# Attention scores as twelve 32-row products in four row groups, in place of four 96-row products

## What is computed

```python
q = _split_heads(query @ Wq.T + bq)
k = _split_heads(key @ Wk.T + bk)
v = _split_heads(value @ Wv.T + bv)
score = jnp.einsum('bhqd,bhkd->bhqk', q, k) * SCALE
attn = jax.nn.softmax(score, axis=-1)
out = jnp.einsum('bhqk,bhkd->bhqd', attn, v)
```

## Time and profile before

| | before |
|---|---|
| median of 3 runs | 1943.54 us (1938.99 to 1945.22) |
| span of the profiled execution | 1941.7 us |
| instructions | 46658 |
| attention, first to last score product | 55.1 us to 1420 us |

### The profile page before, as it was taken

How to read it: one execution, slowest core, us unless ns; L and a number is a source line. 1 busy time by engine, 2 the same in 40 slices (tenths; PEclk the granted TensorE clock), 3 DMA queues, 4 the chain that set the end, 5 groups by cost and what they waited for, 6 DMA issues and landing times. The chain is left out here.

```text
span 1941.7 us, 46658 instructions
## 1 busy us (share of the span) xinstructions
PE 1876.6 (97%) x18832; PEld 1777.8 (92%) x18832; DVE 1468.1 (76%) x2796; ACT 1136.1 (59%) x1921; POOL 652.9 (34%) x643
## 2 busy tenths in 40 slices
PE   7899999999999999999999999999879889999998
PEld 5899999999999999999999999999867789999998
DVE  6777778777777777777777778777788567766667
ACT  2465666666566656666665566656765436665552
POOL 3222223322222323222223232223031126888860
PEclk9899999999999999999999999999989799999999
DMA  8666666666666666666666666667510236666633
GB/s 272 170 155 162 156 174 169 164 157 159 161 153 167 170 167 167 157 158 157 159 167 164 170 165 162 156 163 189 149 60 23 76 118 209 225 220 218 229 115 132
DMA packets 146790, 313.85 MB, mean 162 GB/s; under 512 B 57888, under 2 KB 77216, under 8 KB 143120
## 3 DMA queue, kind: packets, MB, share of 16 engines
q1 hardware_dynamic: 140672, 295.03, 56.2%
q0 software_dynamic: 4752, 13.38, 2.3%
q10 hardware_dynamic: 1152, 2.47, 0.5%
HBM read 134.20 MB, written 18.35 MB: 79 GB/s over the span
## 5 line engine op out<-in xcount | busy, mean ns | idle before, releaser
L453 ACT COPY a_pT<-a_pst 128x512 f32<-128x512 f32 x768 | 421.2, 583 | 409.0 <-PE a_pst L963 409.0
L459 ACT ACTIVATE a_probs<-a_probs,a_nmax 128x1601 f32<-128x1601 f32 x256 | 418.8, 1636 | 140.0 <-DVE a_probs L636 139.8
L636 DVE TENSOR_SCALAR_CACHE_REDUCE a_probs<-a_pss 128x1608 f32<-128x1608 f32 x256 | 467.3, 1825 | 12.8 <-PE a_pss L952 12.3
L963 PE MATMUL a_pst<-a_id,a_probs 128*128 128x128 f32 (+1 forms) x3328 | 452.6, 275 | 13.7 <-ACT a_pT L453 11.5
L963 PEld LDWEIGHTS a_pst<-a_id,a_probs 128*128 128x128 f32 (+1 forms) x3328 | 382.8, 141 | 51.1 <-issue 21.0
L355 POOL TENSOR_TENSOR a_tick<-a_tick 128x1 f32<-128x1 f32 x62 | 12.0, 193 | 953.4 <-DMA a_raw<-in_ctxT 892.1
L654 DVE TENSOR_SCALAR a_khi<-a_psk,a_bk 128x402 fp32r<-128x402 f32 x250 | 158.5, 634 | 142.9 <-PE a_psk L917 141.3
L360 POOL TENSOR_TENSOR a_clo<-a_raw,a_chi 128x402 fp32r<-128x402 f32 x240 | 247.0, 1060 | 4.8
L952 PE MATMUL a_pss<-a_kst,a_bd 96*128 96x402 f32 x1024 | 240.7, 357 | 6.4 <-DVE a_v L661 5.6
L915 PE MATMUL a_pso<-a_whi,a_chi 128*128 128x256 f32 (+1 forms) x806 | 241.9, 300 | 0.0
L917 PE MATMUL a_pso<-a_whi,a_clo 128*128 128x256 f32 (+1 forms) x806 | 227.2, 282 | 0.0
(11 more groups left out here) (251 smaller groups left out, 3511.7 us busy)
## 6 DMA issues: line engine op xcount, KB each, us to landing
a_kst<-a_khi SPq DMA_DIRECT2D x1008, 100.5 KB, 2.6
a_kst<-a_klo SPq DMA_DIRECT2D x504, 100.5 KB, 2.6
a_raw<-in_ctxT SPq DMA_DIRECT2D x60, 804.0 KB, 5.5
f_gur<-in_wgu SPq DMA_DIRECT2D x24, 1408.0 KB, 6.2
f_dr<-in_wd SPq DMA_DIRECT2D x24, 768.0 KB, 7.2
a_bd<-q_scr SPq DMA_DIRECT2D x192, 32.0 KB, 2.0
e_big<-ys_scr SPq DMA_DIRECT2D x8, 512.0 KB, 6.7
a_pT<-in_ctxT SPq DMA_DIRECT2D x2, 1608.0 KB, 9.3
```

The costliest lines, as they stand in the source:

```text
L453: nc.scalar.copy(pT[:, p % HALF, 4 * i:4 * i + 4, :], ps_t[:, i % 2, :].rearrange("p (t q) -> p t q", q=P)).then_inc(t_copied_act, 1)
L459: nc.scalar.activation(pr, pr, ACT.Exp, bias=nmax[:, b, p:p + 1], scale=-1.0, accum_out=esum[:, b, p:p + 1]).then_inc(probs_ready, 1)
L636: nc.vector.tensor_scalar(probs[:, p % 2, :].rearrange("p (b k) -> p b k", b=QK), ps_s[:, :, 0:KQ], -SCALE, None, ALU.mult, ALU.min, accum ...
L963: mm = nc.tensor.transpose(ps_t[0:r, i % 2, (t % 4) * P:(t % 4 + 1) * P], probs[:, p % 2, t * P:t * P + r], a_id_sb[:])
```

## The change

`k_hi` and `k_lo` become the two parts of one tile `k_sb`. The stacked keys become `kq`: row group q (rows 32q to 32q+31) holds key quarter q of each pair, high and low part side by side, 402 columns each. `bd` holds high and low queries side by side, and the same 32 rows in each of the four row groups. `scores` makes three products (high query x high key, high x low, low x high) for each quarter, product by product over the four quarters, each on its own 32 rows and into its quarter's bank, accumulating there.

A batch's key copies go from 48 transfers of 32 rows x 804 columns to 32 of 32 rows x 2 x 402 columns. The queries go from six transfers from memory to four, and three copies of 32 rows x 2048 words (256 KB each) inside the core's memory are added (`spread_queries`), for which SP waits until the four have landed. Two waits of the first batch on stored queries go away, the tiles lie elsewhere in memory, and `bd` is zeroed over 128 rows x 4096 words, where it was 96 x 2048.

```diff
-STACK = 3 * 32
+ROWS = 2 * HD
 PIECES = 2
-COPIES = 16 * 3 * HALF
+COPIES = 16 * (QK // PIECES) * HALF
+PRODUCTS = ((0, 0), (0, 1), (1, 0))
...
-        k_hi, k_lo = sb("a_khi", [P, SKP], F32R), sb("a_klo", [P, SKP], F32R)
+        k_sb = sb("a_k", [P, 2, SKP], F32R)
+        bd = sb("a_bd", [P, 2, 2, PAIRS, P], F32R)
...
-        k_st = sb("a_kst", [STACK, PAIRS, SKP], F32R)
+        kq = sb("a_kq", [P, 2, PAIRS, KQ], F32R)
...
-                for i, part in enumerate((0, 0, 1)):
+                for part in range(2):
                     for e in range(2):
-                        r = 32 * i + HD * e
                         src = q_scr[part, :, bass.ds(n * SQ, SQ)].rearrange("(p e d) t -> e d p t", e=2, d=HD)[e]
-                        sp.dma_start(bd[r:r + HD, slot, :, SQ * e:SQ * (e + 1)].bitcast(F32), src).then_inc(q_loaded, 16)
+                        sp.dma_start(bd[HD * e:HD * (e + 1), slot, part, :, SQ * e:SQ * (e + 1)].bitcast(F32), src).then_inc(q_loaded, 16)
+
+            def spread_queries(n, slot):
+
+                sp.wait_ge(q_loaded, 16 * 4 * (n + 1))
+                for q in range(1, QK):
+                    sp.dma_start(bd[ROWS * q:ROWS * (q + 1), slot].bitcast(F32), bd[0:ROWS, slot].bitcast(F32)).then_inc(q_spread, 16)
...
-                    for i, part in enumerate((k_hi, k_lo, k_hi)):
-                        sp.dma_start(k_st[32 * i:32 * i + 32, HALF * m + j, cols].bitcast(F32),
-                                     part[32 * j:32 * j + 32, cols].bitcast(F32)).then_inc(stacked[m][z], 16)
+                    for q in range(QK // PIECES * z, QK // PIECES * (z + 1)):
+                        sp.dma_start(kq[ROWS * q:ROWS * (q + 1), :, HALF * m + j, :].bitcast(F32),
+                                     k_sb[ROWS * j:ROWS * (j + 1), :, q * KQ:(q + 1) * KQ].bitcast(F32)).then_inc(stacked[m][z], 16)
...
                         load_ctx(n + 2, 0)
+                    if ahead:
+                        spread_queries(n + 1, 1 - b)
...
-                for q in range(QK):
-                    mm = nc.tensor.matmul(ps_s[:, q, 0:KQ], bd[:, b, p, :], k_st[:, p, q * KQ:(q + 1) * KQ], start=True, stop=True)
+                for q_part, k_part in PRODUCTS:
+                    for q in range(QK):
+                        own_rows = slice(ROWS * q, ROWS * (q + 1))
+                        mm = nc.tensor.matmul(ps_s[:, q, 0:KQ], bd[own_rows, b, q_part, p, :], kq[own_rows, k_part, p, :],
+                                              start=(q_part, k_part) == PRODUCTS[0], stop=(q_part, k_part) == PRODUCTS[-1])
                 mm.then_inc(s_filled, 1)
...
-                    pe.wait_ge(q_loaded, 96 * (n + 1))
+                    pe.wait_ge(q_loaded, 16 * 4 * (n + 1))
+                    pe.wait_ge(q_spread, 16 * (QK - 1) * (n + 1))
```

More of the change, by code:

```diff
@@ L117, in attention_and_circuit @@
         c_hi, c_lo = sb("a_chi", [P, 2, NC, SKP], F32R), sb("a_clo", [P, 2, NC, SKP], F32R)
-        k_hi, k_lo = sb("a_khi", [P, SKP], F32R), sb("a_klo", [P, SKP], F32R)
+        k_sb = sb("a_k", [P, 2, SKP], F32R)
+        bd = sb("a_bd", [P, 2, 2, PAIRS, P], F32R)
         with ExitStack() as early:
[L120 to L123, removed]
-        k_st = sb("a_kst", [STACK, PAIRS, SKP], F32R)
+            rowsT = early.enter_context(nc.sbuf_tensor("q_xT", [P, NC, TOK], F32))
+        kq = sb("a_kq", [P, 2, PAIRS, KQ], F32R)
+        q_hi = sb("q_hi", [P, 2, NC, 512], F32R)
+        rows_stats, rows_mv = sb("q_stats", [P, NT, 6]), sb("q_mv", [P, NT, 2])
+        sb("a_gap", [P, 160])
+        with ExitStack() as early:
+            x_sb = early.enter_context(nc.sbuf_tensor("q_x", [P, NT, D], F32))
         v_sb = sb("a_v", [P, 2, KT, D])
@@ L138, in attention_and_circuit @@
         a_id_sb = sb("a_id", [P, P])
-        bd = sb("a_bd", [STACK, 2, PAIRS, P], F32R)
+        q_lo = sb("q_lo", [P, 2, NC, 512], F32R)
         own = sb("a_own", [P, 2])
@@ L158, in attention_and_circuit @@
         w_loaded, w_hi_done, ctx0_hi_done, ctx0_split = sem("a_wl"), sem("a_wh"), sem("a_c0"), sem("a_c0s")
-        const_loaded, first_loaded, ctx_loaded, q_loaded, x_loaded = sem("a_cl"), sem("a_fl"), sem("a_ctxl"), sem("a_ql"), sem("a_xl")
+        const_loaded, first_loaded, ctx_loaded, x_loaded = sem("a_cl"), sem("a_fl"), sem("a_ctxl"), sem("a_xl")
+        q_loaded, q_spread = sem("a_ql"), sem("a_qsp")
         stacked = [[sem(f"a_st{m}{z}") for z in range(PIECES)] for m in range(NC)]
@@ L229, in fill_queries @@
             def fill_queries(n, slot):
-                for i, part in enumerate((0, 0, 1)):
+                for part in range(2):
                     for e in range(2):
-                        r = 32 * i + HD * e
                         src = q_scr[part, :, bass.ds(n * SQ, SQ)].rearrange("(p e d) t -> e d p t", e=2, d=HD)[e]
-                        sp.dma_start(bd[r:r + HD, slot, :, SQ * e:SQ * (e + 1)].bitcast(F32), src).then_inc(q_loaded, 16)
+                        sp.dma_start(bd[HD * e:HD * (e + 1), slot, part, :, SQ * e:SQ * (e + 1)].bitcast(F32), src).then_inc(q_loaded, 16)
[3 more added lines that the diff above has]
+                    sp.dma_start(bd[ROWS * q:ROWS * (q + 1), slot].bitcast(F32), bd[0:ROWS, slot].bitcast(F32)).then_inc(q_spread, 16)
             def stack_keys(n, m, z, of=range(HALF)):
                 sp.wait_ge(kv_copied, STEPS * n + order_of(n).index(("k", m, QK // PIECES * (z + 1) - 1)) + 1)
-                cols = slice(z * SKP // PIECES, (z + 1) * SKP // PIECES)
                 for j in of:
@@ L279, in _ @@
             store_queries(3)
+            spread_queries(0, 0)
             for m in range(NC):
                 for z in range(PIECES):
-                    if (m, z) == (1, 0):
-                        sp.wait_ge(q_stored[1], 32)
-                        sp.wait_ge(q_stored[2], 32 * 2)
                     stack_keys(0, m, z, range(0, HALF, 2))
@@ L498, in stack_first_keys @@
                 act.wait_ge(kv_copied, FIRST_ORDER.index(("k", m, QK // PIECES * (z + 1) - 1)) + 1)
-                cols = slice(z * SKP // PIECES, (z + 1) * SKP // PIECES)
                 for j in range(1, HALF, 2):
-                    for i, part in enumerate((k_hi, k_lo, k_hi)):
-                        act.dma_start(k_st[32 * i:32 * i + 32, HALF * m + j, cols].bitcast(F32),
-                                      part[32 * j:32 * j + 32, cols].bitcast(F32)).then_inc(stacked[m][z], 16)
+                    for q in range(QK // PIECES * z, QK // PIECES * (z + 1)):
+                        act.dma_start(kq[ROWS * q:ROWS * (q + 1), :, HALF * m + j, :].bitcast(F32),
+                                      k_sb[ROWS * j:ROWS * (j + 1), :, q * KQ:(q + 1) * KQ].bitcast(F32)).then_inc(stacked[m][z], 16)
             act.wait_ge(bd_zeroed, 1)
@@ L520, in _ @@
             stack_first_keys(0, 1)
-            for g in (1, 2):
-                act.wait_ge(q_stored[g], 32 * g)
             stack_first_keys(1, 0)
@@ L652, in copy_step @@
                             dve.wait_ge(stacked[1][z], COPIES * n)
-                    hi, lo = (t[:, q * KQ:(q + 1) * KQ] for t in (k_hi, k_lo))
+                    hi, lo = (k_sb[:, part, q * KQ:(q + 1) * KQ] for part in range(2))
                     nc.vector.tensor_scalar(hi, bank[:, 0:KQ], bk_sb[:, m:m + 1], None, ALU.add).then_inc(k_hi_done, 1)
```

## The result

The changed kernel takes 1956.62 us (median of 4 runs, 1952.60 to 1958.77) against 1943.13 us: ratio 1.0068, 95% interval 1.0052 to 1.0085. It is 13.5 us slower, by the interval 10 to 16.5; the forecast's sum was +21.8.

A forecast was written before the change was run, and what follows sets the result against it. The prediction took TensorE's own stream of products to bound the attention. Rounds -43, entry +36 and exit +28 summed to +21.8 us on the 1941.7 us span; with the median 1.8 above it, 1965 us, stated range 1897 to 2010.

The forecast's parts named there:

- What bounds it: In the attention, nothing but TensorE's own stream of products sets the time; TensorE's products are busy 97% of the span.
- Twelve in three rounds: A pair's twelve score products run as three rounds of four, 0.58 us against 0.75, saving 43 us over 256 pairs.
- the nearest row: The earlier trace's price for four column groups, run side by side at 0.11 us a round, taken for row groups too.
- The rivals of serial loads and serial products: In the scores, row groups' weight loads go one behind another, 2147 us, chance 0.11; or products don't overlap, 2390, chance 0.07.
- the second rival: Score rounds slower than one product, 0.244 us each, three 0.73, saving only 4 us; 2004 us, chance 0.08.
- The change of shape: Switching between 128-row products and the pair's scores costs gaps on TensorE: 36 us for entry and 28 for exit.
- Entry: Going into a pair's scores costs 0.09 + 0.10 = 0.19 us, 192 times, 36 us.
- Exit: Going from the scores into the transposes costs 0.09 + 0.06 = 0.15 us, 187 times, 28 us.
- The first rival: No drain between row shapes at the scores, loads hidden as before: -43, 1901 us; chance 0.25 for this family.
- in these the exit hides: Before the transposes, 62 exits with a gap and 7 waiting for exponentials cost nothing; 9 us more if the 62's cover goes.
- Other edits at nothing: Changed key copies, query transfers, three added copies and SP's wait for landed queries, 2.0 us by the median, cost nothing overall.
- for VectorE's last value copy, not for transfers: At the start, TensorE's first scores waited 5.6 us for that copy, so the two waits taken away are worth nothing.

The follow-up runs named there:

- the run in one row group: The changed kernel with all twelve score products on rows 0 to 31; 2387.12 us, ratio 1.2303 to the kernel before.
- The run on 64 rows: The kernel before with each of its four score products on 64 of its 96 rows; 1997.47 us against 1939.73, ratio 1.0288.
- the fifth product: The kernel before with the first quarter's score product made twice, one more product a pair; 1968.65 us against 1939.73, ratio 1.0149.

## Why the prediction was right, and where not

**What bounds it** held: TensorE stayed 97% busy and its waits for other engines did not grow.

**Twelve in three rounds** held, and with it the nearest row: rounds 0.19 us apart, starts of a round within 0.03 us. What four column groups do, four row groups do too. That a full round costs 0.187 us is shown by the run in one row group, 2387 us against 2385 worked out. The rivals of serial loads and serial products are out, and so is the second rival: its rounds were 0.244 us apart.

**The change of shape** held and decides the sign. Entry: 0.09 + 0.10 us as taken from the earlier trace rows. Exit: 0.09 + 0.06 in the pair shown, 0.135 by the medians, against 0.15. The run on 64 rows has this price alone, 57.7 us where 61 were worked out. The first rival, free changes between row shapes, is out. The page TensorEngine Tiling (Array Packing) of the Trainium skill says, in Key Properties, that a change of tiling mode drains TensorE; the 250 gaps agree. What TensorE does in the 0.09 us between the end of a stream and the next load no run shows.

**The step that failed** is "in these the exit hides", the 62 exits with a gap of 0.34 us, which the sum put at nothing. It was called a gap "on no other engine", and it was a wait for ScalarE's copy, shown by the fifth product, which makes it vanish, and by the constant 0.145 us between the end of the copy and the transpose. Such a wait ends at a time that ScalarE sets, so whatever makes TensorE later ahead of it goes into it. These pairs pay the new shape like all others, about 0.15 us in balance, and get back the 0.21 that they had waited. By the starts of all products, a pair at p = 3 or 7 went from 1.26 us (last product ahead of the scores to second transpose) to 1.19, a gain of 0.06 us where a loss of 0.02 was in the sum: 62 x 0.08 = 5 us.

**A second such wait was not seen at all.** At p = 0 of 30 batches the key step behind the eight transposes waited for VectorE's copy of the last key step. Before:

```profile
785.61 1.05 PE L963 MATMUL a_pst<-a_id,a_probs 128*128 128x128 f32 x8
...
785.74 0.64 DVE L656 SCALAR_TENSOR_TENSOR a_klo<-a_psk,a_bk,a_khi 128x402 fp32r<-128x402 f32 x1
...
786.49 0.18 PEld L915 LDWEIGHTS a_psk<-a_chi,a_whi 128*128 128x128 f32 x1
```

This load starts 0.116 to 0.118 us after the end of VectorE's copy (785.74 + 0.64 in the rows) in all 30, and the step's first product 0.14 us after the start of the last transpose. In the changed kernel, and in the runs on 64 rows and with the fifth product, that distance is 0.03 us, the same as at p = 2 and 4 of all four kernels. So the changed kernel gets back 30 x 0.11 = 3.3 us. The profile lists no wait there.

**Sizes.** The 128 pairs at p = 0, 2, 4 and 6 went by the same measure from 1.025 to 1.179 us, +0.154 where the terms gave 0.173, and the 63 behind column products gained 0.038 where they gave 0.017: exit and rounds are each about 0.01 us shorter than I had them. That is 128 x 0.019 + 63 x 0.021 = 3.8 us. The three together are 12 us, of 21.8 - 11.4 = 10.4 us by which the sum was too high in the attention. So the cause of the overshoot is found, and nearly 2 us the other way are not traced.

**The first rival was priced wrong**, though it didn't come. Free changes of shape would not have given 43 us: three products for four give 17. The rest goes into the waits for ScalarE's copy at p = 3 and 7 and for VectorE's at p = 0, where the key step starts 0.31 us behind the last transpose in that run.

**Other edits at nothing**: SP waited for the landed queries 31 times:

```profile
SPq L246 <- DMA a_bd<-q_scr: 41.3, 31, 6.1
```

1.3 us each on average (one of them 6.1), within the 2.0 allowed, and TensorE never waited for keys or queries after the first batch. The start was misread: "for VectorE's last value copy, not for transfers" stops one step early. VectorE itself had waited for the key copies of the first half. Before, and then after:

```profile
46.47 0.64 DVE L654 TENSOR_SCALAR a_khi<-a_pss,a_bk 128x402 fp32r<-128x402 f32 x1 [3.48 <-DMA a_kst<-a_khi]
...
51.35 0.64 DVE L654 TENSOR_SCALAR a_khi<-a_pss,a_bk 128x402 fp32r<-128x402 f32 x1 [2.35 <-DMA a_kst<-a_khi]
```

```profile
47.42 0.64 DVE L659 TENSOR_SCALAR a_k<-a_pss,a_bk 128x402 fp32r<-128x402 f32 x1 [4.40 <-DMA a_kq<-a_k]
...
50.14 0.64 DVE L659 TENSOR_SCALAR a_k<-a_pss,a_bk 128x402 fp32r<-128x402 f32 x1 [0.20 <-DMA a_kq<-a_k]
```

5.8 us of waits became 4.6, and TensorE began 1.2 us earlier. How much of it is the 8 copies a piece in place of 12 and how much the two waits taken away stays open, as said above.

## What to carry to other kernels

Row groups do give four narrow products for the price of one. But going from full rows to part of them and back costs 0.32 us here each time, twice the 0.17 that three rounds save against four products. Count the changes of shape before the rounds; narrow products pay only if enough of them stand together, which no run here tried. And when one engine is busy 99.9% of a stretch, look for the places where it waits anyway, and name them by what ends just before the gap, not by the label it has. They absorb whatever gets longer ahead of them: a step of the right size moved into one of them gained 8.5 us, where larger ones lost 42.

## What the runs showed of the hardware

- Products on 64 rows and on 32 rows pay the same change of shape against 128 rows (first start 0.27 us behind the full product, first transpose 0.27 us behind the scores, in both); 96 against 128 pay none (0.19 us between L917 and L952).
- Products of free row groups start ahead of earlier ones of busy groups: with the products of a quarter directly behind each other the twelve take 0.83 us as before, and the kernel 1958 us against 1957.
- In one row group the twelve narrow products take 0.184 us each, as long as products of 96 or 128 rows.
- A transpose that waits for ScalarE's copy starts 0.144 to 0.146 us after the copy ends, 64 times of 64, and a weight load that waits for VectorE's copy 0.116 to 0.118 us after it, 30 of 30.
